# Third cross attention of a twelve-layer kernel: VectorE's score step is put at the end of the unit before, ahead of the later batches' rows, and one small product moves to ScalarE

## The reference

```python
xn = layer_norm(x, g1, b1)            # context, 8 x 1601 x 256
ln_lat = layer_norm(latents, g2, b2)  # latents, 8 x 64 x 256
q = ln_lat @ Wq
kv = jnp.concatenate([xn, ln_lat], axis=1) @ Wkv      # 1601 + 64 = 1665 keys
...
weight = jnp.einsum('bhld,bhnd->bhln', q * scale, k * scale)
weight = jnp.where(full_mask[:, None, None, :], weight, neg)
weight = jax.nn.softmax(weight, axis=-1)
out = jnp.einsum('bhln,bhnd->bhld', weight, v)
...
return out @ Wout
```

## Time and profile before

| | us |
|---|---|
| median of 3 runs | 2943.83 (2943.23 to 2944.41) |
| profiled execution, own time | 2946.99 |
| its span in the trace | 2945.3 |
| PE busy over the span | 2506.8 (85%) |
| DVE busy over the span | 1761.9 (60%) |
| stretch of the 64 units in the trace | about 1018 to 1832 |

### The profile page before, as it was taken

One profiled execution on the slowest core, in us unless ns is written; L12 is line 12 of the kernel. 1 busy time (PEld: TensorE's weight loads), 2 busy tenths in 40 slices (PEclk: granted clock), 3 DMA queues, 4 the chain that ended last, 5 costly groups with the idle time before them and its releaser, 6 DMA issues. The chain is left out here.

```text
span 2945.3 us, 47037 instructions
## 1 busy us (share of the span) xinstructions
PE 2506.8 (85%) x18669; PEld 1612.2 (55%) x18716; DVE 1761.9 (60%) x3555; ACT 1214.5 (41%) x2131; POOL 972.7 (33%) x561
## 2 busy tenths in 40 slices
PE   8856879999888679999999999569868888888898
PEld 6733546666545355665666665235535555555655
DVE  6976355555482776677666653555574455553577
ACT  3342334444431334444444443234435444443344
POOL 6410223131060343134223400028634334334176
PEclk9977989999999899999999999879979999998999
DMA  3103423333110400100000000013422222220122
GB/s 112 49 1 122 112 64 96 87 87 69 59 36 18 142 1 28 28 1 28 28 28 1 4 1 1 29 52 99 122 58 57 65 65 57 72 58 19 34 90 69
DMA packets 86091, 158.19 MB, mean 54 GB/s; under 512 B 17401, under 2 KB 53970, under 8 KB 85874
## 3 DMA queue, kind: packets, MB, share of 16 engines
q1 hardware_dynamic: 82802, 146.79, 17.4%
q0 software_dynamic: 3072, 8.39, 1.0%
HBM read 115.16 MB, written 0.52 MB: 39 GB/s over the span
## 5 line engine op out<-in xcount | busy, mean ns | idle before, releaser
L3721 PE MATMUL PS<-l2x_rows,l2x_pth 128*128 128x512 f16 x832 | 280.4, 382 | 0.0
L98 PE MATMUL PS<-hot 128*128 128x512 f16 x452 | 132.2, 442 | 133.9 <-DVE l2a_t L2278 48.4
L3722 PE MATMUL PS<-l2x_rows,l2x_ptl 128*128 128x256 f16 x832 | 228.3, 274 | 0.0
L3969 DVE TENSOR_TENSOR l2x_ptl<-PS,l2x_pth 128x512 f16<-128x512 f32 (+1 forms) x256 | 138.9, 584 | 143.2 <-ACT l2x_pth L3817 141.5
L3564 POOL TENSOR_TENSOR l2x_rows<-l2x_rows,l2x_g 128x1024 f32<-128x1024 f32 (+1 forms) x28 | 58.7, 2097 | 454.3 <-DVE l2x_rows L3897 453.7
L3337 DVE CUSTOM_DVE_ANT_0 l1x_junk<-PS,l1x_bias 128x1024 bf16<-128x1024 f32 (+1 forms) x128 | 123.4, 992 | 111.4 <-PE PS L3005 110.6
L3205 ACT ACTIVATE l3x_pT<-PS 128x512 f32<-128x512 f32 (+1 forms) x208 | 122.3, 594 | 152.2 <-PE PS L3051 151.1
L3652 PE MATMUL PS<-l2x_kh,l2x_qth 128*128 128x512 f16 (+1 forms) x512 | 137.0, 351 | 52.1 <-DVE l2x_shift L3917 50.5
L3817 ACT ACTIVATE l2x_pth<-PS 128x512 f16<-128x512 f32 (+1 forms) x256 | 118.4, 514 | 150.3 <-PE PS L3689 149.9
L3337 DVE CUSTOM_DVE_ANT_0 l3x_junk<-PS,l3x_bias 128x1024 bf16<-128x1024 f32 (+1 forms) x128 | 123.7, 992 | 81.2 <-PE PS L3005 80.8
L98 PEld LDWEIGHTS PS<-hot 128*128 128x128 f16 x452 | 46.7, 111 | 208.0 <-DVE l2a_t L2278 49.2
(11 more groups left out here) (864 smaller groups left out, 6719.4 us busy)
## 6 DMA issues: line engine op xcount, KB each, us to landing
l2f_unit<-in_L_ffn_units_dram SPq DMA_DIRECT2D x36, 384.0 KB, 3.1
l3f_unit<-in_L_ffn_units_dram SPq DMA_DIRECT2D x34, 384.0 KB, 3.0
l1x_kst<-l1x_kh SPq DMA_DIRECT2D x128, 100.1 KB, 2.2
l3x_kst<-l3x_kh SPq DMA_DIRECT2D x128, 100.1 KB, 2.2
l2x_rows<-in_ctx_dram SPq DMA_DIRECT2D x8, 1536.0 KB
l1x_ctx<-in_ctx_t_dram SPq DMA_DIRECT2D x7, 1601.0 KB, 7.1
l3x_ctx<-in_ctx_t_dram SPq DMA_DIRECT2D x7, 1601.0 KB, 6.5
l1x_kst<-l1x_kl SPq DMA_DIRECT2D x64, 100.1 KB, 2.2
```

The costliest lines, as they stand in the source:

```text
L98: self.nc.tensor.matmul(self.PS[:, bank, :], self.hot[:, 0:P], self.hot[:], start=True, stop=True)
L3721: nc.tensor.matmul(PS[:, ACC, :], pth[:, m, :], rows2[:, b % 2, m, :, :], start=(m == 0), stop=False)
L3722: last = nc.tensor.matmul(PS[:, ACC, 0:D], ptl[:, m, :], rows2[:, b % 2, m, 0, :], start=False, stop=(m == KT - 1))
L3969: v.tensor_tensor(ptl[:, m[0]:m[0] + len(m), :], PS[:, T_BANK + g % 2, 0:len(m) * P].rearrange("p (m n) -> p m n", n=P), pth[:, m[0]:m[0] ...
```

## The change

VectorE's `weigh` and `score` go from the head of a unit to the tail of the one before, with the units' numbers raised by one, so that both do the same work for the same unit; but the tail is ahead of `beside`, where the old place was behind it. `make_bias` leaves `beside` and stands between `weigh` and `score`. `score(1)` goes to the opening. The product `last_p` becomes an ACTIVATE with `scale=inv` on ScalarE, and ScalarE's `last_means(u)` goes from the head of unit u+1 to the tail of unit u, behind `keep_heads(u-1)`. A new semaphore `last_taken` says that `last_p` has read `sc`; VectorE's `score` of the next unit on the same score tile waits for it instead of for `weighed`.

```diff
                 def last_means(n):
                     act.wait_ge(weighed, n + 1)
+                    nc.scalar.activation(last_p[:], sc[n % 2][:, FULL:FULL + 1], ACT.Copy, scale=inv[:]).then_inc(last_taken, 1)
+                    act.wait_ge(last_taken, n + 1)
...
-                    if u > 0:
-                        last_means(u - 1)
                     high(0)
                     high(1)
...
                     if u > 0:
                         copy_means(u - 1)
                         keep_heads(u - 1)
+                    last_means(u)
                     if r == 1 and b + 1 < B:
                         make_blocks(b + 1)
...
                     if u >= 2:
-                        dve.wait_ge(weighed, u - 1)
+                        dve.wait_ge(last_taken, u - 1)
                     v.memset(tick[:], 0.0)
...
                 def weigh(n):
                     q = n % 2
-                    link(v.reciprocal(inv[:], rsum[:, q:q + 1]))
-                    v.tensor_tensor(last_p[:], sc[q][:, FULL:FULL + 1], inv[:], ALU.mult).then_inc(weighed, 1)
+                    dve.wait_ge(exp_done, n + 1)
+                    v.reciprocal(inv[:], rsum[:, q:q + 1]).then_inc(weighed, 1)
+                    dve.wait_ge(weighed, n + 1)
...
-                    if u > 0:
-                        weigh(u - 1)
-                    if u + 1 < B * R:
-                        score(u + 1)
                     if u > 0:
                         make_means(u - 1)
                     low(0)
                     low(1)
...
                     for group in fills(b, r, 1):
                         prepare(group, b + 1)
+                    weigh(u)
+                    if r == R - 2 and b + 1 < B:
+                        make_bias(b + 1)
+                    if u + 2 < B * R:
+                        score(u + 2)
                     beside(b, r)
```

More of the change, by code:

```diff
@@ L3461, in layer_2_xattn @@
     turned, pt_high, pt_low = (k.sem(f"l2x_{s}") for s in ("turned", "pt_high", "pt_low"))
-    weighed, last_done = k.sem("l2x_weighed"), k.sem("l2x_last_done")
+    weighed, last_taken, last_done = k.sem("l2x_weighed"), k.sem("l2x_last_taken"), k.sem("l2x_last_done")
     sums_made, sums_copied = k.sem("l2x_sums_made"), k.sem("l2x_sums_copied")
@@ L3847, in _ @@
                         unit(b, r)
-                last_means(B * R - 1)
                 copy_means(B * R - 1)
@@ L3947, in beside @@
                     if x < B:
-                        if r == 6:
-                            make_bias(x)
                         if b > 0:
@@ L3998, in _ @@
                     prepare(group, 0, i % FIRST_BANKS)
+                score(1)
                 for b in range(B):
@@ L4001, in _ @@
                         unit(b, r)
-                weigh(B * R - 1)
                 make_means(B * R - 1)
```

## The result

The changed kernel takes 2969.94 us (median of 5 runs, 2962.02 to 2975.54), the kernel before 2943.83 us (2941.16 to 2946.28). The ratio is 1.0088, with a 95% interval of 1.0066 to 1.0109: slower by 26 us. The profiled execution took 2969.94 us, its span is 2968.2 us, 22.9 us longer than the one of before.

What follows compares the result with a forecast made beforehand. PE bounds the layer: its work, waits for VectorE's shift and slow clock. Waits +15.9 (batches 1 to 6) and +8.6 (rest), clock -8 and +2: +18.5 on 2947.0, less 3.2 to the runs' median: 2962 us, range 2946 to 2979.

Steps and rivals of the forecast that it cites:

- Score's start: VectorE's score, waiting for last_p behind keep_heads, starts 3.9 us after turn_means in every unit.
- My 14 waits of 0.1 us: ScalarE's activation at the skill's 0.3 us instead of 0.2: some 14 waits each 0.1 us longer, 1 us in all.
- The new wait of units without a fill: PE ahead of the scores, at r = 0 of each batch and all of batch 7: a new wait of 0.3 us.
- Late work in front of the low halves: VectorE's beside delays means and low halves behind it; PE's turns wait some 45 us for them.
- POOL's lateness: POOL's scaling from r = 7 starts 6.1 us later; PE's K fills wait about 1.1 us, some 12 us in all.
- Batches 1 to 6: PE's waits over these six batches rise from 33.6 to 49.5 us, +15.9, before the clock's -8.
- Batch 7: Last batch: six PE waits of 0.3 us, and 0.7 where its last units wait for low halves.
- Batch 0: First batch: seam waits sum to 21.4 us, within +8.6 for all outside batches 1 to 6; clock adds 2.
- The clock: PE's slow clock behind waits in batches 1 to 6: 8 us remain of 16, so -8; batch 0 +2.
- My mean price of 1.35 us: Slow-clock cost behind a PE wait, 16.2 us over twelve waits, taken for the one long wait left per batch.
- the case "faster": Rival: ScalarE's product comes early, late work starts at 3.7 us after turn_means; about 2890; 0.12 together with weaker forms.
- The price of POOL's hold on the product: Weaker faster rival: last_p on ScalarE escapes POOL's lock, at most 24 us over twelve waits, 2920; within the joint 0.12.

Runs made afterwards that it cites:

- the product early: Changed kernel with last_p on ScalarE ahead of copy_means and keep_heads, and VectorE's weigh ahead of the fills of place 1: 2905.04 us, ratio 0.9821.
- The extra moments: Forty bn_stats of finished tiles added at r = 3 and 4, batches 1 to 5: changed kernel 2997.12 us, ratio 1.0135; kernel before 2962.69 us, ratio 1.0014.
- each half alone: Changed kernel with last_p back on VectorE (order alone): 2934.18 us, ratio 0.9911; kernel before with only last_p on ScalarE: 2925.2 us, ratio 0.9881.

## Why the prediction was right

The forecast was 2962 us, range 2946 to 2979, slower; measured 2969.94. The mechanism is the one forecast: the score waits for the product behind the kept heads, the late work behind it delays the low halves and POOL, and PE waits there. The size was too small, +18.5 us forecast, where the profiles differ by 22.9 and the medians by 26.

- **Score's start.** Forecast at 3.9 us after `turn_means`; it is 1588.21 - 1584.15 = 4.06, and 1.53 with the product early. The kept heads end 3.59 after it, as forecast (3.65), but from there to the score pass 0.47 us, not 0.25. `last_p` takes 0.294 us, where I took 0.2 from a 128x4 activation; the Trainium skill's budget of about 0.3 us for an activation (ScalarE: Activation LUTs, Rules for kernel authors) was the better figure, and the trace agrees. (My 14 waits of 0.1 us by that page are 1.4 us, not 1.) Making the score wait for the kept heads again takes the ratio from 0.9821 to 1.0038, so this step is shown.
- **The new wait of units without a fill.** Forecast 0.3 us; the profile shows idle times of 0.33, but a unit of batch 7 is 0.5 us longer, 11.13 for 10.62.
- **Late work in front of the low halves.** Forecast were waits of the turns of some 45 us; they are 48.6. At r = 1 I forecast 2.9: there are 2.72 idle and 0.2 more inside the turns, where the last of them waits for the second low half (five turns take 0.93 us for 0.71). The extra moments show that no cover is left.
- **POOL's lateness.** Forecast were twelve waits of 1.1 us; there are 9.9 us in twelve waits, 0.82 to 0.84 each. Those twelve vanish with the early product.
- **The terms that were too small.** Batches 1 to 6 were to lose 15.9 us to waits and get 8 back from the clock, 7.9 in all; they lost 13.0. In batches 4 and 5 the clock stayed at full speed through a whole batch and it took 102.45 us (`turn_means` at 1468.73 to 1571.18 in batch 4), 10.3 more than the 92.1 of PE's work, where I had summed waits of 9.0. So the waits were 0.1 to 0.3 us too short at each seam but r = 5, for one part because of the later start of the score. Batch 7 likewise lost 3.8, not 2.5. Batch 0 lost 7.3, where 8.1 were forecast (8.6 and 2, less batch 7's 2.5). That leaves 24.1 us in the layer where 18.5 were forecast.
- **The clock.** Forecast was that 8 of 16 us stay, spread over all six waits of r = 1. Four of the six waits brought a slow clock and two didn't, which makes 5.3 us in these four seams; the mean rose to 0.99. So somewhat more came back than forecast, and the waits cost that much more. My mean price of 1.35 us was near the 1.2 to 1.4 of each of the four, but nothing in the forecast says which waits bring it.
- **The rivals.** The mechanism that I gave for the case "faster", a product that comes early on ScalarE (2890), is real; the kernel that does it has ratio 0.9821, which on 2943.8 is 2891. I was right that the code as changed doesn't do it. The price of POOL's hold on the product (at most 24 us, 2920) was real as well: the product on ScalarE in the order before has ratio 0.9881. In the changed kernel the product isn't held either, but the late start of the score costs more than that.

Not settled: why the clock fell behind some waits of 2.7 us and not behind others. It goes with the spread of the changed kernel's runs: their mean granted clock over the whole program is 0.942 in the fastest (2962.02 us) and 0.937 in the slowest (2975.54), with the other three in order between them. Whether the clock makes all of that spread isn't shown.

## What to carry to other kernels

When a step is pulled forward on one engine, ask what it now waits for: here a wait for a small product at the tail of another engine's queue undid the move, and each half alone was worth 26 to 35 us. Put the small instruction that others wait for ahead of those that themselves wait, not behind them: with the product and the reciprocal early, a loss of 26 us became a gain of 53. And work that goes out of the way of one deadline goes in the way of the next, so compare the cover at both places before moving it.

## What the runs showed of the hardware

A VectorE product of 128 numbers was held for 4.98 us behind one GpSimd instruction of 5.74 us, and went on as that ended; on ScalarE the same product took 0.294 or 0.295 us in all 64 units of the changed kernel, also where GpSimd was in the same instruction (product at 1189.27, GpSimd from 1185.18 to 1190.92), and 0.285 to 0.298 us with the product early. An activation of one column with a scale from memory (0.294 us) takes longer than the one of four columns (0.205 us); that the scale is the reason was not tried. Waits of TensorE of the same length, 2.71 or 2.72 us, at the same place of the program, were followed by a fall of the granted clock (0.62 to 0.69 over the next 4 us) in four batches and by none (1.00) in two.
